# Another order for the steps of the tree block, between the scan and the layers

## The chip, the cores and the metric

The kernel runs on one core of a Trainium2 chip. The metric is the device time of one execution in microseconds, the median of three runs. The core has five engines with a queue of instructions each: TensorE (PE, matrix products), VectorE (DVE), ScalarE (ACT), GpSimd (POOL), and SyncE (SP), which here only starts transfers. An engine takes its instructions strictly in the order in which the program wrote them; between engines only semaphores hold. So an instruction whose input is late holds up everything written behind it on the same engine, ready or not. That is what this case is about.

## The reference, cut to what matters

Four blocks, each `x = x + layernorm(block(layernorm(x)))`, on 2048 tokens (8 sequences of 256) of width 128:

```python
x = x + _layernorm(_L0_attn_ref(_layernorm(x), ...))   # selective scan ("Mamba"), then a norm with gain and bias
x = x + _layernorm(_L0_ffn_ref(_layernorm(x), ...))    # the tree block
x = x + _layernorm(_L1_attn_ref(_layernorm(x), ...))   # four retention layers
x = x + _layernorm(_L1_ffn_ref(_layernorm(x), ...))    # eight experts, one chosen per token
```

The tree block, which the change reorders:

```python
gate = sigmoid(q_flat @ routers.T)                     # 255 gates per token
for level in range(8):                                 # 256 leaf probabilities, products along the paths
    g = gate[:, n - 1:2 * n - 1]
    lp = lp * stack([1 - g, g])
ret = leaf_prob @ leaf_values
out = ret @ Wout_w.T + Wout_b
```

## The kernel before, in words

The 2048 tokens are worked on in four groups of 512 (g = 0 to 3). The scan runs from about 100 us to 280 us of the span. Then comes the list `OPENING`: all steps of the tree block for the four groups, and behind them, interlaced, the first steps of the first retention layer. Each entry is (step, part, group). Every engine walks through the same list and issues its own part of a step, if it has one. So the list alone sets each engine's order: the four engines' programs differ from it only by leaving steps out.

The list is the sorted list of the times `g + t`, where `t` comes from a table: `TREE_SCHEDULE` (L193) for the tree steps, `SCHEDULE` (L173), shifted by 13.25, for the layer's. The numbers have no meaning to the chip. They are only sorted.

The steps of one group, in the order in which each needs the one before it. In brackets the engines and the lines:

- `y_proj` (PE L1230), `t1` (DVE adds, and takes means and variances, L894 to L898; POOL makes reciprocal roots, L519, L521): the end of the scan block.
- `g_norm` (DVE L1017, L1021), `g_stats` (DVE statistics, POOL L528 to L533), `o_norm` (ACT normalises, L757; POOL adds to X, L607).
- `b_stats` (DVE, POOL L528 to L533), `b_norm` (ACT L757), `b_turn` (PE transposes, L1223; ACT copies out, L771).
- `logits` (PE L1372, eight passes; ACT sigmoid, L775), `low_levels` (POOL, levels 0 to 4 of the tree, L592 to L446; in group 0 a memset follows, L600), `levels` (DVE, levels 5 to 7, L444 and L446).
- `lp` (PE transposes the leaves, L1384; ACT copies out, L779), `b_proj` (PE L1230; DVE adds the bias, L1041).
- `t2_stats` (DVE, POOL), `t2_norm` (ACT L757; POOL adds to X, L610), `rx_stats` (DVE, POOL), `rx_norm` (ACT L757).
- Then the first layer: `stats1` and `norm1` (DVE L909, POOL L519, L521), `turn1` (PE L1223, ACT L792), `rotate` (PE L1416, DVE L1076), `spread` (POOL L624, ACT L814), `gate`, `keys`, `scores` (PE L1445, DVE L1091), `values`, `states`, `mix` (PE L1472 ends it), `gather` (ACT L826), `heads` (PE L1480, DVE L1107 to L1111), `var` (DVE L1115, L1117; POOL L629), `unit` (DVE L1122), and so on.

Two waits matter beside those of data. PE's first `rotate` waits until DVE has added the bias of all four groups (`pe.wait_ge(t2_ready, G)`), because it writes to the same PSUM banks. And PE's `b_turn` and `logits` wait for ACT to have emptied their banks, two groups back. After `OPENING` the layers go on in the order `LAYER`, which the change doesn't touch.

Of the kernel before, what the change touches and what calls it, by code (L numbers as in the profile page):

```python
# [180 lines left out]
def layer_order():  # L181
# [9 lines left out]


TREE_SCHEDULE = (  # L193
    (-0.363, "y_proj"), (1.902, "t1"), (4.537, "g_norm"), (4.577, "g_stats"), (5.451, "o_norm"), (6.325, "b_stats"),
    (6.568, "b_norm"), (7.126, "b_turn"), (7.946, "logits"), (7.780, "low_levels"), (8.920, "levels"), (9.756, "lp"),
    (10.296, "b_proj"), (11.612, "t2_stats"), (11.986, "t2_norm"), (12.840, "rx_stats"), (12.992, "rx_norm"),)
FIRST_STEPS_AT, FIRST_STEPS_SCALE = 13.25, 1.00
TREE_STEPS = {what for _, what in TREE_SCHEDULE}
OPENING = [(what, k, g, 0) for _, what, k, g in sorted(
# [1426 lines left out]
```

## Time and profile before

| what | value |
|---|---|
| median of 3 runs | 772.23 us (769.97 to 772.78) |
| the profiled execution's own time | 776.75 us |
| its span | 774.7 us |
| PE busy | 657.1 us, 85% |
| DVE busy | 621.8 us, 80% |
| POOL busy | 428.7 us, 55% |
| ACT busy | 415.2 us, 54% |

The share of busy time is an average over stages with different limits. The page's chain of waits is no help here: it follows the last instruction back and its shares round to 0% on every engine. The timelines of the single engines are what can be read. A row of a timeline gives the start and the length of a group of instructions, and in square brackets how long the engine idled before it and who ended that.

### The profile page before, as it was taken

The numbers are of one execution on the slowest core, as the hardware profiler recorded it, in microseconds if no ns is written. First come the engines' busy times: TensorE is split into PE (matmuls) and PEld (weight loads), VectorE is DVE, ScalarE is ACT, GpSimd is POOL, SyncE is SP. The second block draws the span as 40 slices with busy tenths as digits, with TensorE's granted clock in tenths as the row PEclk, the third lists the DMA queues.
The fourth block names the chain that finished last, engine by engine and source line by source line (L and its number), as shares of the span: only waits on it lengthen the run. The fifth ranks groups of instructions, "written<-read, shape, count | busy, mean of one in ns | idle before, by whom it ended". The sixth has DMA issues, their size and how long they took to land. (4 is left out here: it accounts for less than half of the span.)

```text
span 774.7 us, 13076 instructions
## 1 busy us (share of the span) xinstructions
PE 657.1 (85%) x4791; PEld 438.3 (57%) x4800; DVE 621.8 (80%) x1519; ACT 415.2 (54%) x729; POOL 428.7 (55%) x380
## 2 busy tenths in 40 slices
PE   3997798898988863657889999999999999788894
PEld 1435444444444442554667777777777777566673
DVE  6479898998989857376778888888888888768686
ACT  1996776785767506445545444444444444444451
POOL 6113587795877747655565555555555556443112
PEclk9997799999999995697999999999999999999997
DMA  9003133333333300000000000000000000000001
GB/s 323 10 5 54 34 100 87 89 99 82 76 89 81 81 2 0 0 1 0 2 1 22 2 5 15 22 2 4 15 22 1 6 16 2 1 1 0 1 27 30
DMA packets 17296, 27.34 MB, mean 35 GB/s; under 512 B 2320, under 2 KB 7056, under 8 KB 16976
## 3 DMA queue, kind: packets, MB, share of 16 engines
q1 hardware_dynamic: 17232, 26.51, 12.5%
q8 instruction: 38, 0.62, 0.3%
q14 instruction: 26, 0.21, 0.1%
HBM read 25.32 MB, written 1.18 MB: 34 GB/s over the span
## 5 line engine op out<-in xcount | busy, mean ns | idle before, releaser
L582 POOL TENSOR_TENSOR arena<-arena 128x1024 f32<-128x1024 f32 x64 | 149.9, 2360 | 56.7 <-PE psum L1331 39.4
L1000 DVE TENSOR_TENSOR_SCAN arena<-arena,psum 128x1024 f32<-128x1024 f32 x64 | 142.1, 2269 | 4.2 <-PE psum L1314 2.3
L1331 PE MATMUL psum<-arena,Cs 128*128 128x512 f32 x256 | 125.3, 613 | 1.2 <-POOL arena L582 1.2
L519 POOL TENSOR_TENSOR ve<-mv,eps 128x4 f32<-128x4 f32 x52 | 15.9, 305 | 181.7 <-DVE mv L898 181.7
L714 ACT ACTIVATE arena<-arena 128x510 f32<-128x510 f32 x128 | 84.8, 710 | 54.2 <-DVE arena L1000 52.3
L629 POOL TENSOR_TENSOR arena<-arena,mhalf 128x32 f32<-128x32 f32 x16 | 86.8, 5426 | 2.4 <-DVE arena L1117 2.4
L1331 PEld LDWEIGHTS psum<-arena,Cs 128*128 128x128 f32 x256 | 46.3, 196 | 47.5 <-issue 36.0
L1223 PE MATMUL psum<-Cs,arena 128*128 128x128 f32 x240 | 40.4, 294 | 37.4 <-ACT arena L757 23.2
L1223 PEld LDWEIGHTS psum<-Cs,arena 128*128 128x128 f32 x240 | 29.3, 149 | 56.9 <-ACT arena L757 24.6
L1416 PE MATMUL psum<-arena,Wl 128*128 128x512 f32 x128 | 60.2, 614 | 1.6 <-issue 1.6
L1230 PEld LDWEIGHTS psum<-Wl,arena 128*128 128x128 f32 x384 | 46.6, 191 | 20.9 <-DVE arena L1126 13.3
L1230 PE MATMUL psum<-Wl,arena 128*128 128x128 f32 x384 | 49.7, 279 | 10.0 <-DVE arena L1126 10.0
L1314 PE MATMUL psum<-Cs,arena 128*128 128x128 f32 x256 | 37.0, 293 | 23.5 <-ACT arena L736 20.6
L1314 PEld LDWEIGHTS psum<-Cs,arena 128*128 128x128 f32 x256 | 31.9, 151 | 42.4 <-issue 37.4
L521 POOL TENSOR_TENSOR rs<-ve,mhalf 128x4 f32<-128x4 f32 x52 | 52.6, 1012 | 4.1
L736 ACT ACTIVATE arena<-arena 128x256 f32<-128x256 f32 x128 | 54.1, 493 | 0.0
L894 DVE BATCH_NORM_STATS2 st<-arena 128x6 f32<-128x128 f32 x208 | 45.2, 280 | 3.6 <-ACT arena L757 2.3
L1230 PEld LDWEIGHTS psum<-Wd,arena 128*128 128x128 f32 (+1 forms) x320 | 40.4, 195 | 12.1 <-issue 7.9
L624 POOL TENSOR_TENSOR arena<-arena 128x512 f32<-128x512 f32 x32 | 45.8, 1450 | 2.6 <-DVE arena L1076 2.6
L838 ACT ACTIVATE arena<-psum,Lnc 128x512 f32<-128x512 f32 x16 | 12.4, 778 | 64.4 <-PE psum L1223 64.4
L1206 DVE SCALAR_TENSOR_TENSOR arena<-psum,arena 128x128 f32<-128x128 f32 x128 | 35.9, 344 | 13.0 <-PE psum L1230 11.5
L909 DVE TENSOR_SCALAR arena<-arena,mv,rs 128x128 f32<-128x128 f32 x160 | 44.6, 342 | 1.7 <-POOL rs L521 1.7
(172 smaller groups left out, 1395.5 us busy)
## 6 DMA issues: line engine op xcount, KB each, us to landing
arena<-c_rows_by_state SPq DMA_DIRECT2D x32, 512.0 KB, 4.8
Wl<-wl SPq DMA_DIRECT2D x4, 384.0 KB, 3.1
Wd<-wd SPq DMA_DIRECT2D x1, 1100.0 KB, 10.8
X<-x SPq DMA_DIRECT2D x4, 256.0 KB, 6.7
Sel<-sel SPq DMA_DIRECT2D x1, 1024.0 KB, 8.7
Wl<-wl SPq DMA_DIRECT2D x4, 256.0 KB, 2.8
out<-X SPq DMA_DIRECT2D x4, 256.0 KB, 2.3
Cs<-const SPq DMA_DIRECT2D x1, 614.0 KB, 9.4
```

What stands on the lines that cost most here:

```text
L521: pool.tensor_tensor(rs[:, g * GT:(g + 1) * GT], ve[:, g * GT:(g + 1) * GT], mhalf[:, 0:GT], ALU.pow).then_inc(rstd_ready, 1)
L582: pool.tensor_tensor(Hc[:, h], Hs[:, r, h], Crows[:, r], ALU.mult).then_inc(hc_ready, 1)
L624: pool.tensor_tensor(dst[:, half], halves[:, 0, half], halves[:, 1, half], ALU.add).then_inc(summed.sem, 1)
L629: pool.tensor_tensor(gst[:, cols], gst[:, cols], mhalf[:], ALU.pow).then_inc(rstd_ready, 1)
L714: ins = act.activation(Da[:, h, group(e)].rearrange(seq, s=S)[:, :, 1:], Dt[:, h, group(g)].rearrange(seq, s=S)[:, :, 1:], ACT.Exp, scale= ...
L736: ins = act.activation(Wslot[n % 2][:, part, k, :], Flip[g % 2][:, k * 256:(k + 1) * 256], ACT.Identity, scale=Bt_rows[:, column:column + 1])
L1000: dve.tensor_tensor_scan(Hs[:, turn % 2, h], Da[:, h], rows_of(turn, h), 0.0, ALU.mult, ALU.add).then_inc(scanned, 1)
L1223: ins = pe.transpose(dst[:, tile(k)], src3[:, g * GT + k, :], ident)
L1230: ins = pe.matmul(dst[:, k * width:(k + 1) * width], r[:, tile(k)], w, start=i == 0, stop=i == len(rows) - 1)
L1314: ins = pe.transpose(rows[:, tile(e * GT + k)], Wslot[slot % 2][:, e, k, tile(h)], ident)
L1331: ins = pe.matmul(bank[h], ident, Hc[:, h, group(e)], start=False, stop=False, skip_group_check=True)
L1416: pe.matmul(claim(what, k, layer, g), Wl[:, WL["qk"]][:, tile(k)], Ht[:, group(g)], start=True, stop=True).then_inc(proj.sem, 1)
```

## The change

`TREE_SCHEDULE` has other numbers. Nothing else is changed: the instructions are the same, with the same tiles, and only the order within each engine's queue differs. The new table has one line more, so every line number below it is one higher in the changed kernel. The table begins so, before and after:

```diff
 TREE_SCHEDULE = (
-    (-0.363, "y_proj"), (1.902, "t1"), (4.537, "g_norm"), (4.577, "g_stats"), (5.451, "o_norm"), (6.325, "b_stats"),
+    (0.519, "y_proj"), (1.829, "t1"), (4.728, "g_norm"), (4.819, "g_stats"), (5.661, "o_norm"), (6.453, "b_stats"),
```

ACT, at the tree's start, before. L757 from `X` is `b_norm`, L757 from `arena` is `o_norm`, L771 the copy of `b_turn`, L775 the sigmoid of `logits`, L779 the copies of `lp`. The twelve rows run from the copy of `b_turn` 0 to the copies of `lp` 0.

```order
L771 COPY arena<-psum 128x512
L757 ACTIVATE arena<-arena,shift,rs 128x128 x4
L757 ACTIVATE arena<-X,shift,rs 128x128 x4
L775 ACT_TABLE_LOAD
L775 ACTIVATE arena<-psum 128x512 x2
L771 COPY arena<-psum 128x512
L757 ACTIVATE arena<-arena,shift,rs 128x128 x4
L757 ACTIVATE arena<-X,shift,rs 128x128 x4
L775 ACTIVATE arena<-psum 128x512 x2
L771 COPY arena<-psum 128x512
L757 ACTIVATE arena<-X,shift,rs 128x128 x4
L779 COPY arena<-psum 128x512 x2
```

The same place of the changed kernel (L758, L772, L776 and L780 are those lines):

```order
L758 ACTIVATE arena<-arena,shift,rs 128x128 x4
L772 COPY arena<-psum 128x512
L776 ACT_TABLE_LOAD
L776 ACTIVATE arena<-psum 128x512 x2
L758 ACTIVATE arena<-X,shift,rs 128x128 x4
L758 ACTIVATE arena<-arena,shift,rs 128x128 x4
L772 COPY arena<-psum 128x512
L776 ACTIVATE arena<-psum 128x512 x2
L758 ACTIVATE arena<-X,shift,rs 128x128 x4
L780 COPY arena<-psum 128x512 x2
L772 COPY arena<-psum 128x512
L776 ACTIVATE arena<-psum 128x512 x2
```

The sigmoid of a group now stands ahead of the next group's `b_norm`, where it stood behind it. `o_norm` of group 2 stands ahead of the first `b_turn` copy, `b_norm` of group 1 and `o_norm` of group 3 stand behind the first sigmoid. On PE `lp` of group 0 goes ahead of `b_turn` 2, and `b_proj` 0 and `lp` 1 ahead of `b_turn` 3. POOL's order is the same all through the tree block.

DVE, where the tree's last bias sum meets the layer's first norm, before. L1041 is the bias sum of `b_proj` 3, L894 from `X` is `rx_stats` 1, from `arena` are `stats1` 0 and `t2_stats` 2, L909 is `norm1` 0, L1076 `rotate` 0:

```order
L1041 TENSOR_TENSOR arena<-psum,Wb 128x512
L894 BN_STATS st<-arena 128x6 x4
L896 MEMSET scratch 128x1
L898 BN_AGGR mv<-st 128x2 x4
L894 BN_STATS st<-arena 128x6 x4
L896 MEMSET scratch 128x1
L898 BN_AGGR mv<-st 128x2 x4
L909 TENSOR_SCALAR arena<-arena,mv,rs 128x128 x4
L894 BN_STATS st<-X 128x6 x4
L896 MEMSET scratch 128x1
L898 BN_AGGR mv<-st 128x2 x4
L1076 TENSOR_TENSOR arena<-psum,Cs 128x512 x4
```

And after, from `t2_stats` 2 on:

```order
L895 BN_STATS st<-arena 128x6 x4
L897 MEMSET scratch 128x1
L899 BN_AGGR mv<-st 128x2 x4
L910 TENSOR_SCALAR arena<-arena,mv,rs 128x128 x4
L895 BN_STATS st<-X 128x6 x4
L897 MEMSET scratch 128x1
L899 BN_AGGR mv<-st 128x2 x4
L1042 TENSOR_TENSOR arena<-psum,Wb 128x512
L1077 TENSOR_TENSOR arena<-psum,Cs 128x512 x4
```

The last bias sum (L1041, now L1042) stood ahead of all this and now stands right ahead of `rotate` 0, behind `norm1` 0 and `rx_stats` 1. That of group 2 has moved in the same way, from ahead of `t2_stats` 1 to behind `rx_stats` 0.

POOL, where the first layer's `var` 0 (L629) meets `rx_stats` 3 (L528 to L533) and `spread` (L624), before:

```order
L629 TENSOR_TENSOR arena<-arena,mhalf 128x32
L528 TENSOR_TENSOR ve<-mv,eps 128x4
L529 TENSOR_TENSOR shift<-zeros,mv 128x4
L531 TENSOR_TENSOR rs<-ve,mhalf 128x4
L533 TENSOR_TENSOR shift<-shift,rs 128x4
L624 TENSOR_TENSOR arena<-arena 128x512 x2
```

And after, L529 to L534 being `rx_stats` 3:

```order
L529 TENSOR_TENSOR ve<-mv,eps 128x4
L530 TENSOR_TENSOR shift<-zeros,mv 128x4
L532 TENSOR_TENSOR rs<-ve,mhalf 128x4
L534 TENSOR_TENSOR shift<-shift,rs 128x4
L630 TENSOR_TENSOR arena<-arena,mhalf 128x32
L625 TENSOR_TENSOR arena<-arena 128x512 x2
```

The four small operations of `rx_stats` 3 stand ahead of the root of `var` 0 instead of behind it. DVE's part has moved in the same way. `rx_stats` 2 has moved ahead of the second `scores` of group 0 on DVE.

## Rows read from the trace of the kernel before

**Rows 1.** Stretch, length, PE, PEld, DVE, ACT, POOL busy (count), PEclk, DMA share, GB/s.
```profile
290.00:352.57 62.57, 30.77 (x149) 25.39 (x149) 39.43 (x182) 30.58 (x67) 42.27 (x100) 0.69 0.00 1
...
400.00:660.00 260.00, 251.90 (x2784) 192.78 (x2784) 224.09 (x613) 125.40 (x211) 146.92 (x95) 1.00 0.04 10
```

**Rows 2.** Timeline of ACT, 302 to 339 us: start, length, what, idle before.
```profile
302.81 1.65 ACT L757 ACTIVATE arena<-arena,shift,rs 128x128 f32<-128x128 f32 x4
...
306.27 1.28 ACT L775 ACT_TABLE_LOAD   x1
...
315.93 1.65 ACT L757 ACTIVATE arena<-X,shift,rs 128x128 f32<-128x128 f32 x4 [5.28 <-POOL shift L533]
317.49 1.05 ACT L775 ACTIVATE arena<-psum 128x512 f32<-128x512 f32 x2
...
323.99 1.65 ACT L757 ACTIVATE arena<-X,shift,rs 128x128 f32<-128x128 f32 x4 [4.62 <-POOL shift L533]
...
326.49 1.08 ACT L775 ACTIVATE arena<-psum 128x512 f32<-128x512 f32 x2
...
332.68 0.60 ACT L775 ACTIVATE arena<-psum 128x512 f32<-128x512 f32 x1 [0.26 <-PE psum L1372]
...
338.35 1.65 ACT L757 ACTIVATE arena<-arena,shift,rs 128x128 f32<-128x128 f32 x4 [2.38 <-POOL shift L533]
```

**Rows 3.** Timeline of PE, 301 to 353 us.
```profile
301.18 1.12 PE L1223 MATMUL psum<-Cs,arena 128*128 128x128 f32 x4 [16.01 <-ACT arena L757]
302.97 3.78 PE L1372 MATMUL psum<-Wrq,arena 128*128 128x256 f32 x8 [0.68 <-ACT arena L771]
...
318.54 1.92 PE L1384 MATMUL psum<-Cs,arena 128*128 128x128 f32 x8
...
325.69 0.79 PE L1223 MATMUL psum<-Cs,arena 128*128 128x128 f32 x4 [2.35 <-ACT arena L757]
326.64 3.40 PE L1230 MATMUL psum<-Wlv,arena 128*128 128x128 f32 x16 [0.16 <-ACT arena L779]
...
330.75 1.89 PE L1372 MATMUL psum<-Wrq,arena 128*128 128x256 f32 x8
332.48 1.95 PE L1230 MATMUL psum<-Wlv,arena 128*128 128x128 f32 x16
...
352.57 2.04 PE L1416 MATMUL psum<-arena,Wl 128*128 128x512 f32 x2 [0.92 <-issue]
```

**Rows 4.** Timelines of POOL and DVE, 308 to 315 us.
```profile
308.73 0.20 POOL L592 TENSOR_TENSOR arena<-ones,arena 128x4 f32<-128x4 f32 x1 [1.25 <-ACT arena L775]
...
311.74 0.29 DVE L444 TENSOR_TENSOR arena<-arena 128x128 f32<-128x128 f32 x1 [4.61 <-POOL arena L446]
...
314.04 0.72 DVE L446 TENSOR_TENSOR arena<-arena 128x512 f32<-128x512 f32 x1
```

**Rows 5.** Two stretches with another granted clock; columns as in rows 1.
```profile
322.40:325.80 3.40, 1.05 (x5) 0.62 (x4) 2.12 (x4) 1.81 (x5) 1.48 (x2) 0.96 0.00 0
325.80:329.20 3.40, 3.24 (x16) 2.87 (x17) 0.00 (x0) 2.24 (x5) 1.20 (x6) 0.54 0.00 0
```

**Rows 6.** Timeline of DVE, 343 to 351 us.
```profile
343.55 0.69 DVE L1041 TENSOR_TENSOR arena<-psum,Wb 128x512 f32<-128x512 f32 x1 [0.88 <-PE psum L1230]
...
350.34 0.86 DVE L894 BATCH_NORM_STATS2 st<-X 128x6 f32<-128x128 f32 x4
```

**Rows 7.** Timelines of POOL, ACT, PE and DVE, 383 to 394 us.
```profile
383.09 5.43 POOL L629 TENSOR_TENSOR arena<-arena,mhalf 128x32 f32<-128x32 f32 x1 [2.35 <-DVE arena L1117]
388.48 0.20 POOL L528 TENSOR_TENSOR ve<-mv,eps 128x4 f32<-128x4 f32 x1
...
390.67 2.48 POOL L624 TENSOR_TENSOR arena<-arena 128x512 f32<-128x512 f32 x2
...
390.75 1.65 ACT L757 ACTIVATE arena<-X,shift,rs 128x128 f32<-128x128 f32 x4 [6.96 <-POOL shift L533]
...
392.92 0.66 PE L1480 MATMUL psum<-Cs,arena 128*128 128x128 f32 x4 [2.24 <-ACT arena L826]
...
393.61 0.69 DVE L1107 TENSOR_REDUCE arena<-psum 128x32 f32<-128x512 f32 x1 [4.32 <-PE psum L1480]
```

More of the change, by code:

```diff
@@ L193 @@
 TREE_SCHEDULE = (
-    (-0.363, "y_proj"), (1.902, "t1"), (4.537, "g_norm"), (4.577, "g_stats"), (5.451, "o_norm"), (6.325, "b_stats"),
-    (6.568, "b_norm"), (7.126, "b_turn"), (7.946, "logits"), (7.780, "low_levels"), (8.920, "levels"), (9.756, "lp"),
-    (10.296, "b_proj"), (11.612, "t2_stats"), (11.986, "t2_norm"), (12.840, "rx_stats"), (12.992, "rx_norm"),)
+    (0.519, "y_proj"), (1.829, "t1"), (4.728, "g_norm"), (4.819, "g_stats"), (5.661, "o_norm"), (6.453, "b_stats"),
+    (7.238, "b_norm"), (7.973, "b_turn"), (8.202, "logits"), (8.299, "low_levels"), (9.328, "levels"),
+    (9.813, "lp"), (10.784, "b_proj"), (11.604, "t2_stats"), (11.914, "t2_norm"), (12.693, "rx_stats"),
+    (13.007, "rx_norm"),)
 FIRST_STEPS_AT, FIRST_STEPS_SCALE = 13.25, 1.00
```

## The prediction

> **What bounds the kernel now.** I read the busy times by stretch first, then the timeline of each engine over the tree block, then the granted clock there, last the timelines around 390 us. From 290 to 352.57 us, the stretch that is reordered up to the first `rotate`, no engine is the bound: POOL, the busiest, works 42.3 of 62.6 us and PE 30.8. From 400 to 660 us PE works 251.9 of 260 us [rows 1]. So the tree block is a chain of waits between four engines, and what it gives up or takes moves the PE-bound layers behind it by the same amount: their order and their work stay as they are.
>
> In the tree block the reader is to see where ACT stands still with work ready behind it. At 315.93 ACT has waited 5.28 us for POOL's shift, to do `b_norm` 2. Behind it stands the sigmoid of group 1, which starts only at 317.49. At 323.99 it is the same: 4.62 us of wait for the shift of `b_norm` 3, with the copies of `lp` 0 and the sigmoid of group 2 (326.49) behind it [rows 2]. This late sigmoid makes POOL's `low_levels` 2 late, but what counts most is the last one. Sigmoid 3 ends at 332.68 + 0.60 = 333.28. POOL then has the low levels of group 3, and only behind them, in its fixed order, `t2_stats` 0, for whose shift ACT waits until 338.35 [rows 2]. From there one chain of group 0 runs through `t2_norm`, `rx_stats`, `rx_norm`, `stats1`, `norm1` and `turn1` to `rotate` at 352.57 [rows 3]. POOL's order is not changed, so the end of sigmoid 3 is the point by which the tree block is to be judged.
>
> **The change, part by part.** All times are on the clock of the profiled execution of before.
>
> First group. ACT now does `o_norm` 2 (1.65 us) ahead of the copy of `b_turn` 0. It started at 302.81 behind that copy and could have started little before, since POOL's shift had just come; I take 302.6. It ends at 304.3, and the copy (about 0.6, a sigmoid's length) at 304.9, where it was done by 302.97, when PE began: 1.9 later [rows 2, 3]. The logits take 3.78 at the low clock [rows 3] and end at 308.7. The table load (1.28 us [rows 2]) waits for nothing and lies beside them. The second sigmoid ends at 309.3. Before, POOL started on it at 308.73 [rows 4]. So group 0 is 0.6 late: low levels 309.3 to 312.3 (3.0, from 308.73 to 311.74), `levels` 312.3 to 315.3 (3.0, from 311.74 to 314.76) [rows 4].
>
> Second group. `b_norm` 1 now follows the sigmoid: 309.3 to 311.0, 4.7 later than before. Transposes 1.12 [rows 3], to 312.1. Meanwhile ACT does `o_norm` 3, to 312.6, then the copy, to 313.2. Logits 3.78, to 317.0. The sigmoid isn't queued behind a wait any more and ends at 317.6. Before, it ended at 317.49 + 1.05 = 318.54 [rows 2]. The group has lost 4.7 us and still comes out 0.9 earlier, since the head start was spent waiting.
>
> Third group. Shift 2 comes 0.6 late, as the low levels before it, at 316.5, ahead of need. `b_norm` 2 runs 317.6 to 319.2. PE turns the leaves of group 0 meanwhile, 317.0 to 318.9 at the low clock (1.92 [rows 3]). `b_turn` 2 and its copy: 320.7 at the high clock (0.79), 321.0 at the low (1.12) [rows 3]. Logits 1.89 or 3.78 [rows 3]: 322.6 or 324.8. Sigmoid 2 ends at 323.2 or 325.4, before at 327.57 [rows 2].
>
> Fourth group. Shift 3 is due on POOL behind the low levels of group 1, which start at 317.75 instead of 318.6, so at 323.1 instead of 323.96 [rows 2]. `b_norm` 3 comes behind sigmoid 2 and ends at 324.9 or 327.1. PE fills the time with `b_proj` 0 (1.95 at the high clock [rows 3]) and `lp` 1 (about 1.0, half of 1.92), from 322.6 to 325.5 or from 324.8 to 327.7. Then `b_turn` 3 (0.79), copy (0.6), logits (1.89), sigmoid (0.6): 325.5 + 3.9 = 329.4, or 327.7 + 3.9 = 331.6. Before: 333.28 [rows 2]. So the tree term is **-3.9 us** if logits 2 run at 2.4 GHz and **-1.7 us** if they run at 1.2 GHz. I take -3.0, nearer the first: in the new order PE is busy from 313.2 to 318.9 almost without a break just before.
>
> From there to `rotate` 0 the same steps lie in the same order, but for the bias sums. The sum of group 3 (0.69) was done at 343.55 in idle time. Now it stands behind `rx_stats` 1, which starts at 350.34 and takes 1.2 [rows 6]. So it would run from 351.55 to 352.25, and PE's `rotate`, which waits for it, started at 352.57 [rows 3]. It fits with 0.3 us to spare: cost 0, the cover being `turn1` on PE and ACT. If `rx_stats` 1 slips by more than 0.3, every further 0.1 counts. From above, the whole sum and its statistics would cost 0.69 + 1.2 = 1.9; from below nothing can be gained. The sum of group 2 moves behind `rx_stats` 0, where DVE waits for ACT's `rx_norm` anyway: 0.
>
> `rx_stats` 2 ahead of the second `scores`: DVE does the same two pieces in the other order ahead of the same third one, and `mix`, the next to need the mask, comes later. 0.
>
> `rx_stats` 3. Before, its POOL part stood behind the root of `var` 0 (5.43 us from 383.09), its shift came at 390.7, and ACT did `rx_norm` 3 from 390.75 to 392.3, with `gather` 1 behind it. PE had finished `mix` 1 at 392.92 - 2.24 = 390.68 and stood 2.24 us; DVE stood 4.32 [rows 7]. Now the shift comes 2.2 us (388.48 to 390.67) after DVE's 383.3, ACT does `rx_norm` 3 in its idle 6.96 us, `gather` runs from 390.7 to 391.3 and `heads` 1 start at 391.35: 1.57 earlier. The price is the root, which moves behind the four small operations: 385.4 to 390.9, and `spread` (390.67) starts at 390.9, 0.2 later [rows 7]. ACT's copies for `scores` hang on that, so not all of the 1.57 comes through. Alone `gather` would let them follow directly. Bounds 0 and -1.6, I take **-1.1**.
>
> **Sum.** -3.0 - 1.1 = -4.1 us. The profiled execution's own time is 776.75, so 772.65. That execution is 4.5 above the median of the runs shown, and the change is the same in both: 772.23 - 4.1 = **768.1 us**.
>
> **The clock.** What decides inside the tree term is PE's clock. Between 322.4 and 325.8 the granted clock was 0.96, nearly all of it at 2.4 GHz, while PE worked 1.05 us of 3.4. Then it was 0.54, nearly all at 1.2 GHz, though PE was busy for 3.24 of the next 3.4 us [rows 5]. The same `b_proj` took 3.40 in it and 1.95 later [rows 3]. The break before the fall that the row shows was 2.35 us [rows 3]. In the new order the breaks after 313.2 are a few tenths to 1.2 us, and no such break is left until the last leaves.
> The Trainium skill speaks against a change that spreads PE's work out at the start (TensorE: Matmul & The Clock Gate, section Why this matters for your kernels): breaks between bursts of matmuls take the clock down, and it advises to keep them short. The trace agrees, with 3.40 against 1.95 for the same products.
> By that rule the new breaks at 302 to 313 (2.6, 2.4 and 1.1 us by the times above) keep the clock low longer; by the trace it was low there before as well. What it would do later is the first rival.
>
> **Rivals.**
> 1. The clock stays low through logits 2 and `b_proj` 0. Tree term: -1.7 + (3.40 - 1.95) = -0.3; with -1.1 that is 770.8. For it: the first logits come in two separate bursts. Against: PE is busier from 317 on than before. Chance 0.17.
> 2. The gain at 390 us doesn't come, since the root of `var` 0 and `spread` are what `scores` 2 wait for: only -3.0, 769.2. Chance 0.1.
> 3. Slower. The low clock holds from the first logits to the last: logits 2 to 324.8, `b_proj` 0 to 328.2, `lp` 1 to 330.1, `b_turn` 3 to 331.2, copy 331.8, logits 3 to 335.6, sigmoid 336.2. That is 2.9 later than 333.28; with -1.1 it is +1.8, and with `rx_stats` 1 slipping as well up to +1.9 more: 774.0, at most 776. It decides as soon as sigmoid 3 ends 1.1 later than before. For it: `b_turn` 1 is 4.7 late. Against: busy times like those here brought the clock up before. Chance 0.07.
> 4. Nothing comes through, because another step of the chain to `rotate` 0 is bound by something that hasn't moved: 772.2. In the trace each step there waits for the one before. Chance 0.08.
>
> **How the numbers follow.** The forecast has 0.58, with 766.5 to 770.1 as its own range: the two ends of the tree term with the -1.1, -5.0 and -2.8, and 0.7 of scatter in a median of three, a quarter of the 2.8 between the runs shown. A difference of under 0.5%, 3.9 us here, can't be told from none. Of the forecast two thirds lie below 768.4, which is 0.38, and a third of rival 2, 0.03, and 0.02 for a gain that I don't see: faster 0.43. Slower by over 0.5% needs the far end of rival 3: 0.05. The rest, 0.52, is the same. The range runs from 766.0 to 772.3, with rivals 1, 2 and 4 in it and rival 3 outside.
>
> **What would show it.** Right: sigmoid 1 ends at about 317.6 with no ACT wait for a shift ahead of it; logits 2 take 1.9; sigmoid 3 ends at 329.4 to 331.6; `rotate` 0 starts near 349.6 right behind `turn1`; DVE's last bias sum ends before it; ahead of `heads` 1 PE stands under 1 us. Wrong: a logits row of 3.8 us after 320; a wait of PE for DVE's L1042 ahead of `rotate` 0; ACT waiting for a shift with a sigmoid behind it; a break of over 1.5 us between the two kernels' starts of the layers that isn't there at 353.

## The result, and the profile after

The changed kernel takes 768.59 us (median of 18 runs, 765.06 to 770.12), the kernel before 771.54 (18 runs beside them). The ratio is 0.9953, with a 95% interval of 0.9935 to 0.9971: 3.6 us less by the ratio, 2.95 by the two medians. The interval lies below 1, so the change does save time; the gain is just under the half percent up to which the prediction speaks of the same. A gain of 4.1 us was forecast. The same kernel in a second set (12 runs, experiment e7 below) came out at 0.9972 (0.9957 to 0.9987), 2.2 us less by the ratio.

| | before | after |
|---|---|---|
| median | 771.54 | 768.59 |
| profiled execution, own time | 776.75 | 769.43 |
| its span | 774.7 | 767.6 |
| PE, DVE, POOL, ACT busy | 657.1, 621.8, 428.7, 415.2 | 651.6, 622.2, 429.2, 415.3 |

The two traces differ by 7.1 us of span, twice what the times say. So distances, and not absolute times, have to be compared. The first transposes of the tree block (`b_turn` 0) start at 301.18 before and at 299.42 after. These 1.76 us lie in the scan, whose code and order are the same in both, so they are no gain of the change: in the thirteen traces used here `b_turn` 0 starts anywhere from 294.9 to 301.2. Another 1.7 us of the 7.1 lie behind `heads` 14, again in the same code and order; that stretch takes 122.5 to 127.0 us over the thirteen traces. I count from `b_turn` 0. Busy time by stretch, as in [rows 1]:

```profile
290.00:352.57 62.57, 34.54 (x154) 26.09 (x155) 39.06 (x173) 33.06 (x73) 42.99 (x100) 0.69 0.00 1
...
400.00:660.00 260.00, 249.67 (x2785) 191.97 (x2787) 222.22 (x610) 124.25 (x209) 149.03 (x94) 0.99 0.04 10
```

The first window is that of before, and the layer begins 5 us earlier here. In the stretch that matches it, 288.24 to 347.56, PE works 29.5 of 59.3 us and POOL 42.0. So in the tree block no engine is the bound, as before, and in the layers PE is. Timeline of ACT, answering to [rows 2]:

```profile
300.85 1.65 ACT L758 ACTIVATE arena<-arena,shift,rs 128x128 f32<-128x128 f32 x4 [1.49 <-POOL shift L534]
302.40 0.56 ACT L772 COPY arena<-psum 128x512 f32<-128x512 f32 x1
...
306.83 0.60 ACT L776 ACTIVATE arena<-psum 128x512 f32<-128x512 f32 x1 [1.11 <-PE psum L1373]
...
314.84 0.60 ACT L776 ACTIVATE arena<-psum 128x512 f32<-128x512 f32 x1 [1.11 <-PE psum L1373]
315.33 1.64 ACT L758 ACTIVATE arena<-X,shift,rs 128x128 f32<-128x128 f32 x4
...
321.65 0.60 ACT L776 ACTIVATE arena<-psum 128x512 f32<-128x512 f32 x1 [1.11 <-PE psum L1373]
322.14 1.63 ACT L758 ACTIVATE arena<-X,shift,rs 128x128 f32<-128x128 f32 x4
...
328.03 0.60 ACT L776 ACTIVATE arena<-psum 128x512 f32<-128x512 f32 x1 [0.26 <-PE psum L1373]
...
333.51 1.65 ACT L758 ACTIVATE arena<-arena,shift,rs 128x128 f32<-128x128 f32 x4 [2.19 <-POOL shift L534]
```

The waits of 5.28 and 4.62 us for POOL's shift are gone: `b_norm` 2 and 3 (315.33 and 322.14) follow their sigmoids without a wait. What ACT waits for now, between the sigmoids, is PE. One wait for a shift is left at the start, 1.49 us ahead of `o_norm` 2, with the copy of `b_turn` 0 behind it. Timeline of PE, answering to [rows 3]:

```profile
299.42 1.11 PE L1224 MATMUL psum<-Cs,arena 128*128 128x128 f32 x4 [16.01 <-ACT arena L758]
303.01 3.78 PE L1373 MATMUL psum<-Wrq,arena 128*128 128x256 f32 x8 [2.49 <-ACT arena L772]
...
318.45 3.16 PE L1373 MATMUL psum<-Wrq,arena 128*128 128x256 f32 x8 [0.78 <-ACT arena L772]
321.41 2.50 PE L1231 MATMUL psum<-Wlv,arena 128*128 128x128 f32 x16
...
326.00 1.99 PE L1373 MATMUL psum<-Wrq,arena 128*128 128x256 f32 x8 [0.78 <-ACT arena L772]
...
347.56 6.50 PE L1417 MATMUL psum<-arena,Wl 128*128 128x512 f32 x8 [0.91 <-DVE arena L1042]
```

Logits 2 ran partly at the low clock in this execution: 3.16 us, between 1.9 and 3.8, with a granted clock of 0.61 from 318.45 to 321.60. DVE's moved bias sums:

```profile
337.75 0.66 DVE L1042 TENSOR_TENSOR arena<-psum,Wb 128x512 f32<-128x512 f32 x1
...
345.33 0.86 DVE L895 BATCH_NORM_STATS2 st<-X 128x6 f32<-128x128 f32 x4
...
346.53 0.66 DVE L1042 TENSOR_TENSOR arena<-psum,Wb 128x512 f32<-128x512 f32 x1
```

And the timelines of POOL, ACT, PE and DVE around `heads` 1, answering to [rows 7]:

```profile
380.86 5.43 POOL L630 TENSOR_TENSOR arena<-arena,mhalf 128x32 f32<-128x32 f32 x1
386.25 2.94 POOL L625 TENSOR_TENSOR arena<-arena 128x512 f32<-128x512 f32 x2
...
380.94 1.65 ACT L758 ACTIVATE arena<-X,shift,rs 128x128 f32<-128x128 f32 x4 [1.43 <-POOL shift L534]
...
387.10 0.66 PE L1481 MATMUL psum<-Cs,arena 128*128 128x128 f32 x4 [0.70 <-ACT arena L827]
...
390.10 0.63 PE L1224 MATMUL psum<-Cs,arena 128*128 128x128 f32 x4 [1.48 <-DVE arena L1112]
...
386.32 1.74 DVE L1123 TENSOR_TENSOR arena<-arena 128x512 f32<-128x512 f32 x1 [1.91 <-POOL arena L630]
387.98 0.68 DVE L1108 TENSOR_REDUCE arena<-psum 128x32 f32<-128x512 f32 x1
```

PE stands 0.70 instead of 2.24 us ahead of `heads` 1 (L1481). In its place one wait is new and one is longer: DVE's `unit` 0 waits 1.91 us for the later root, and then takes 1.74 us beside POOL's `spread`; PE waits 1.48 us for DVE's L1112, where it was 0.96 before.

The points of the chain, each as its distance from `b_turn` 0 in the trace, before and after, in us. `heads` are DVE's (L1107), the end of rotate 0 is that of DVE's fourth product:

| point | before | after | difference | second trace after (e7) |
|---|---|---|---|---|
| sigmoid 0 ends | 7.48 | 8.01 | +0.53 | +0.53 |
| sigmoid 1 ends | 17.36 | 16.02 | -1.34 | -1.34 |
| sigmoid 2 ends | 26.39 | 22.83 | -3.56 | -4.73 |
| sigmoid 3 ends | 32.10 | 29.21 | -2.89 | -4.54 |
| rotate 0 starts | 51.39 | 48.14 | -3.25 | -4.46 |
| rotate 0 ends | 57.89 | 55.37 | -2.52 | -4.09 |
| heads 1 | 92.43 | 88.56 | -3.87 | -5.44 |
| heads 2 | 110.96 | 107.43 | -3.53 | -5.10 |

From there to `heads` 14 the difference stays within 0.1 us in the first trace and in e7's. In others it changes by up to 0.6 us (e5's, from -3.60 to -3.04).

### The profile page after: what moved, and what is told of

Same layout as the page of the kernel before. It is cut to its first block and busy times, and to the rows that moved or that the text cites. A ratio compares the mean times of both kernels' runs of the same rounds, so it can differ in the third digit from the quotient of the medians.

```text
span 767.6 us, 13076 instructions
## 1 busy us (share of the span) xinstructions
PE 651.6 (85%) x4791; PEld 434.7 (57%) x4800; DVE 622.2 (81%) x1519; ACT 415.3 (54%) x729; POOL 429.2 (56%) x380
## 5 line engine op out<-in xcount | busy, mean ns | idle before, releaser
L1077 DVE TENSOR_TENSOR arena<-psum,Cs 128x512 f32<-128x512 f32 x64 | 40.3, 688 | 5.2 <-PE psum L1417 5.2
```

## The experiments

All ratios are against the kernel before, run on the same chip. They were run in three sets of four.

**e1: the tree block's moves alone.**

```diff
+put_ahead(('rx_stats', 0, 2, 0), ('states', 0, 0, 0))
+put_ahead(('rx_stats', 0, 3, 0), ('states', 0, 1, 0))
```

(in the changed kernel, behind the list `OPENING`; `put_ahead` takes an entry out and puts it ahead of another)

> The changed kernel with rx_stats 2 and 3 put back where they stood (behind the second scores of their layer group and behind var 0). My theory: two separate gains, some 2.5 us in the tree block and some 1 us ahead of heads 1. So here the tree gain alone: 2.5 us below the kernel before (ratio 0.9968), rotate 0 early as in the changed kernel, but ACT's rx_norm 3 again ahead of gather 1 and PE idle 2.2 us ahead of heads 1. Rival (the whole gain is the tree's, the move of rx_stats is neutral): 3.6 us below before.

Measured: 767.25 us, ratio 0.995 (0.9932 to 0.9968), 3.9 us less and as good as with the moves of `rx_stats`. In the trace sigmoid 3 ends 4.66 us earlier than before, counted from `b_turn` 0, the rotate ends 4.46 earlier, and from `heads` 0 to `heads` 2 it takes 36.2 us as before (35.2 in the changed kernel). So the tree moves carry all of the gain that the times show.

**e2 and e8: `rx_stats` 3 alone.**

```diff
+put_ahead(('rx_stats', 0, 3, 0), ('var', 0, 0, 0))
```

(in the kernel before; the same kernel twice)

> The kernel before with one move alone: rx_stats 3 ahead of var 0 (on DVE and POOL). My theory: 1.0 us below before; PE idle ahead of heads 1 down from 2.24 to 0.7, heads 1 on PE 1.5 earlier, of which about 0.5 is given back because unit 0 and so out_turn 0 wait for the root of var 0. Rival: 0, because the root that now comes 2 us later decides instead.

> The kernel before with rx_stats 3 alone ahead of var 0, once more. Its first trace shows 35.2 us from heads 0 to heads 2 where before shows 36.2, but its times came out 0.1% above before, in two clusters, 768 to 770 and 772 to 775. Theory: the 1.0 us is real and the upper cluster is a fall of the clock somewhere, which the move doesn't cause: ratio 0.9985 or within 0.2% of it, and the same 35.2 us. Rival: the later root brings a break of PE in which the clock falls more often, which costs what the move gains: ratio again 1.000 or above, and if the trace is of the upper cluster, a low clock near heads 1.

Measured: e2 772.21 us, ratio 1.001 (0.9989 to 1.003); e8 771.36 us, ratio 0.9996 (0.9972 to 1.002). One execution of e8, the profiled one, took 3655 us. The cause isn't known, and its trace is not used. In e2's trace `heads` 0 to 2 take 35.2 us, 1.0 less than before. That distance is 36.2 in the traces of before, e1 and e9, without the move, and 35.2 in the nine with it (e3, also without it, had 38.6 with the fall of the clock shown below). So the 1.0 us is in every trace, and the times don't show it: e8's interval includes 0.9987, e2's just does not.

The granted clock of the single executions, averaged over their span, shows more. Divided at 0.952, the executions of e2 and e8 without the one of 3655 us, and the 75 of the kernel before in the three sets, fall so:

| | at 0.952 or less | median of these | above 0.952 | median of these |
|---|---|---|---|---|
| before | 17 of 75 | 774.0 us | 58 | 770.7 us |
| e2 and e8 | 15 of 23 | 772.3 us | 8 | 768.4 us |

At a like clock the kernel with the move is about 2 us faster, but most of its executions run at the lower clock, and that can eat the gain. It speaks for e8's rival. With the tree moves it points the same way: e1's five executions, without the move, have 0.954 to 0.955, and the 37 of the changed kernel, e7 and e10, with it, have 0.943 to 0.952. Where in the span the clock is lost, and whether the later root does it, is not shown: e2's trace is one of the high clock (0.957).

**e3: only the two sigmoids ahead of the waits.**

```diff
+put_ahead(('logits', 0, 1, 0), ('b_norm', 0, 2, 0))
+put_ahead(('b_turn', 0, 2, 0), ('b_norm', 0, 3, 0))
+put_ahead(('logits', 0, 2, 0), ('b_norm', 0, 3, 0))
```

(in the kernel before)

> The kernel before with two moves alone: the sigmoid of group 1 ahead of b_norm 2, and logits 2 with its sigmoid ahead of lp 0 and b_norm 3. Nothing of groups 0 and 1 is delayed as in the changed kernel. If the two sigmoids queued behind a wait for a shift are the whole tree gain: sigmoid 3 ends 2.9 us earlier against the first transposes than before, time 2.5 us below before. My theory gives a little less, 1.5 us, since b_proj 0 and lp 1 still stand behind b_turn 3 on PE and lp 0's copies behind b_norm 3 on ACT.

Measured: 770.87 us, ratio 0.9997 (0.9977 to 1.0016). In the trace sigmoid 3 is 1.61 us earlier than in the trace of before, but only 0.26 earlier than in e2's, whose tree block has the old order. The two are not alike in the clock, though. Logits 2 took 2.23 us in e2's trace, and here the full 3.78, behind a break of 5.68 us:

```profile
314.15 1.11 PE L1233 MATMUL psum<-Cs,arena 128*128 128x128 f32 x4 [5.68 <-ACT arena L767]
315.94 3.78 PE L1382 MATMUL psum<-Wrq,arena 128*128 128x256 f32 x8 [0.68 <-ACT arena L781]
```

So up to 1.5 us of what the sigmoids gave may have gone to the clock in this execution. Windows of e3 around `heads` 1, columns as in [rows 1]:

```profile
382.70:389.50 6.80, 4.33 (x81) 2.88 (x79) 2.41 (x6) 3.55 (x8) 4.90 (x7) 0.94 0.01 2
389.50:396.30 6.80, 6.30 (x45) 5.66 (x47) 4.80 (x17) 3.67 (x7) 1.54 (x2) 0.56 0.00 0
```

The clock fell to the lower level at 389.5, behind the break of 2.24 us ahead of `heads` 1, and `heads` 1 to 2 took 20.96 us instead of 18.53. The same break, as long, is in the trace of before, and there it stayed high:

```profile
388.10:394.90 6.80, 4.10 (x81) 2.88 (x79) 2.42 (x6) 3.78 (x8) 4.89 (x7) 1.00 0.01 2
```

So by time the sigmoids alone bring nothing. Whether that is because they gain little, or because this order loses to the clock what it gains, one trace can't tell.

**e9: the sigmoids, and `lp` and `b_proj` ahead of the next `b_turn`.**

```diff
+put_ahead(('logits', 0, 1, 0), ('b_norm', 0, 2, 0))
+put_ahead(('lp', 0, 0, 0), ('b_turn', 0, 2, 0))
+put_ahead(('b_turn', 0, 2, 0), ('b_norm', 0, 3, 0))
+put_ahead(('lp', 0, 0, 0), ('b_turn', 0, 2, 0))
+put_ahead(('logits', 0, 2, 0), ('b_norm', 0, 3, 0))
+put_ahead(('b_proj', 0, 0, 0), ('b_turn', 0, 3, 0))
+put_ahead(('lp', 0, 1, 0), ('b_turn', 0, 3, 0))
```

(in the kernel before)

> The kernel before with PE's and ACT's new order from logits 1 on (sigmoid 1 ahead of b_norm 2, lp 0 ahead of b_turn 2, b_proj 0 and lp 1 ahead of b_turn 3, sigmoid 2 ahead of b_norm 3), but the old one ahead of it, so groups 0 and 1 are not delayed, and DVE and POOL as before. Theory: the tree gain of the changed kernel comes from these moves and not from the early ones, which only cost 0.5 us at sigmoid 0; sigmoid 3 is 3 to 4.5 us earlier against the first transposes than before, 2.5 to 3 us in time, ratio 0.9965. Rival: the sigmoids moved alone brought nothing in time (ratio 0.9997), and so won't these: above 0.9985.

Measured: 767.61 us, ratio 0.995 (0.9928 to 0.9973). Its interval doesn't meet e3's. So these moves, from logits 1 on, are the change's gain; `o_norm` 2 ahead of the first copy and DVE's moves add nothing that shows. Its trace is one with a low clock for logits 2, 3.78 us, as in e3's. Between these two, alike in that, sigmoid 3 is 0.97 us earlier here; the ratios are 3.6 us apart, and the rest is in neither trace. Sigmoid 3 is 2.57 us earlier than before:

```profile
302.91 1.99 PE L1386 MATMUL psum<-Wrq,arena 128*128 128x256 f32 x8 [1.58 <-ACT arena L785]
308.54 1.91 PE L1398 MATMUL psum<-Cs,arena 128*128 128x128 f32 x8 [3.63 <-DVE arena L460]
311.36 1.11 PE L1237 MATMUL psum<-Cs,arena 128*128 128x128 f32 x4 [0.92 <-ACT arena L771]
313.15 3.78 PE L1386 MATMUL psum<-Wrq,arena 128*128 128x256 f32 x8 [0.68 <-ACT arena L785]
316.73 2.99 PE L1244 MATMUL psum<-Wlv,arena 128*128 128x128 f32 x16
```

**e10: DVE's bias sums back.**

```diff
+put_ahead(('b_proj', 0, 1, 0), ('t2_stats', 0, 0, 0))
+put_ahead(('b_proj', 0, 2, 0), ('t2_stats', 0, 1, 0))
+put_ahead(('b_proj', 0, 3, 0), ('stats1', 0, 0, 0))
```

(in the changed kernel)

> The changed kernel with DVE's three moved bias sums (b_proj 1, 2, 3) back where they stood; PE, ACT and POOL as changed. Theory: they cost and bring nothing, PE starts rotate 0 at the same distance behind turn1 0 (2.0 us): ratio as the changed kernel, 0.995 to 0.997. Rival: the last sum right ahead of the rotate holds it by some tenths of a microsecond: then rotate 0 starts up to 0.3 us earlier here.

Measured: 767.35 us, ratio 0.9932 (0.9905 to 0.996), not to be told from the changed kernel's. The start of the rotate is 2.00 us behind `turn1` 0 in both (343.55 to 345.55 here, 345.56 to 347.56 there). The row of PE names DVE's sum as what ended its wait in the changed kernel (0.91), and here nothing (0.92, "issue"), at the same distance: a name alone doesn't make a wait.

**e4: PE kept busy ahead of the first layer.**

```diff
+                if (step[0], step[2]) == ("turn1", 0):
+                    pe.wait_ge(gated, 2 * G)
+                    keep_busy(bank[2], 12)
```

(in the changed kernel, in PE's loop over its steps; the definition of `keep_busy` is cut. It issues so many products of 128x256 whose result is read by nobody. The rows show each as two passes: x24 is 12 products.)

> The changed kernel with 12 more products of 128x256 on PE (their result is read by nobody) ahead of turn1 0, in the 6.9 us in which PE idles there. Theory: PE's granted clock fell in that idle time, so the first rotate ran at 1.2 GHz (6.5 us for 8 passes against 3.6 later). With PE busy there the clock stays at 2.4 GHz, the rotate takes about 3.7 and the layers start 2.5 us earlier: 2.5 us below the changed kernel, ratio to before about 0.992. Rival: DVE's four sums and the bias sum bind the rotate, not the clock: under 0.7 us.

Measured: 767.95 us, ratio 0.9936 (0.9912 to 0.996). In its trace:

```profile
334.87 5.34 PE L1508 MATMUL psum<-Wrq 128*128 128x256 f32 x24
341.93 0.63 PE L1224 MATMUL psum<-Cs,arena 128*128 128x128 f32 x4 [1.72 <-DVE arena L910]
343.61 3.70 PE L1417 MATMUL psum<-arena,Wl 128*128 128x512 f32 x8 [1.05 <-DVE arena L1042]
```

The first rotate takes 3.70 instead of 6.50 us, and from its start to DVE's fourth product it takes 4.43 instead of 7.23: 2.8 us in these two traces, as the theory has it, and the rival falls there. By time it was less: 4.9 us below before, where the changed kernel had 3.6, with intervals that overlap. The trace is that of the fastest execution. The three fastest, 761.2 to 763.9 us, had a granted clock of 0.959 to 0.965 over their span; the other eight, 765.3 to 769.4, had 0.952 to 0.956, near the changed kernel's 0.948 to 0.952. So in most executions the products seem to have held the clock up only a little.

**e5: PE kept busy at the start of the tree block.** 28 such products ahead of `b_turn` 0, 4 ahead of logits 0 and 3 ahead of `b_turn` 1, in bank 7.

```diff
+            busy = {('b_turn', 0): 28, ('logits', 0): 4, ('b_turn', 1): 3}
+                if (step[0], step[2]) in busy:
+                    keep_busy(bank[7], busy[step[0], step[2]])
```

(in the changed kernel, in PE's loop over its steps, like e4's; lines between these are cut)

> The changed kernel with 35 more products of 128x256 on PE (read by nobody) where it idles at the start of the tree block: 28 ahead of the first transposes, 4 ahead of logits 0, 3 ahead of b_turn 1. Theory: the clock then stays at 2.4 GHz from the end of the scan, logits 0 and 1 take 1.9 us each instead of 3.8, sigmoid 3 ends 2.8 us earlier against the first transposes than in the changed kernel, and the time falls by 2.5 us (ratio to before about 0.992). Rival: POOL's low levels, its memset and its statistics bind from sigmoid 0 on, and at most the 1.9 us of logits 0 come through; or the tree block doesn't care and it is 0.

Measured: 768.63 us, ratio 0.9966 (0.9942 to 0.999): nothing gained on the changed kernel. The trace says why:

```profile
308.80 2.00 PE L1373 MATMUL psum<-Wrq,arena 128*128 128x256 f32 x8 [1.35 <-ACT arena L772]
311.38 1.09 PE L1385 MATMUL psum<-Cs,arena 128*128 128x128 f32 x8 [0.58 <-DVE arena L447]
314.20 1.11 PE L1224 MATMUL psum<-Cs,arena 128*128 128x128 f32 x4 [1.73 <-ACT arena L758]
315.99 3.78 PE L1373 MATMUL psum<-Wrq,arena 128*128 128x256 f32 x8 [0.68 <-ACT arena L772]
```

Logits 1 went fast (2.00) and sigmoid 1 ended 3.47 us earlier than before. Then PE had to wait for `levels` and for `b_norm` 2, the clock fell (0.93 from 311.0 to 314.2, then 0.50 to 320), and logits 2 took 3.78: all of it was given back. Sigmoid 3 is 2.92 us earlier than before, where the changed kernel has 2.89 in its first trace and 4.54 in its second. The products ahead of logits 0 also ran over their break at the low clock (3.62 us together) and held it up.

**e6: both.** The products of e5 and e4, with 14 ahead of `turn1` 0 and one ahead of the first rotate.

```diff
+            busy = {('b_turn', 0): 28, ('logits', 0): 4, ('b_turn', 1): 3}
+                    keep_busy(bank[7], busy[step[0], step[2]])
+                if (step[0], step[2]) == ("turn1", 0):
+                    keep_busy(bank[2], 14)
+                if (step[0], step[2]) == ("rotate", 0):
+                    keep_busy(bank[2], 1)
```

(in the changed kernel; lines between these are cut)

> The additional products of e5 and those of e4 together, with 14 instead of 12 ahead of turn1 0 and one ahead of the first rotate. Theory: both add up, 5 us below the changed kernel, ratio to before 0.989. The runs of e4 lay in two clusters, 761 to 766 and 768 to 769; if that is the clock falling in the gap in some executions, the two more products make the upper cluster smaller. Rival: the gains overlap, no better than the better of the two.

Measured: 762.52 us, ratio 0.9915 (0.9887 to 0.9944). In the trace sigmoid 3 is 6.12 us earlier than before and the rotate's end 8.01. The clusters are 760.8 to 765 (six runs) and 769 (two). By the ratios of the same set it is 4.4 us below the changed kernel (e7). Alone, e4 gave 1.3 us and e5 0.5 by their ratios; e6 also has three more products than the two together, and what share is theirs wasn't tested.

**e11: products in all larger breaks, in the changed order.**

```diff
+            busy = {('b_turn', 0): 35, ('logits', 0): 2, ('b_turn', 1): 4,
+                    ('logits', 1): 1, ('b_turn', 2): 1, ('logits', 2): 1}
```

(the rest as e6)

> The changed kernel with additional products (read by nobody) in all larger breaks of PE: 35 ahead of b_turn 0, 2 ahead of logits 0, 4 ahead of b_turn 1, 1 each ahead of logits 1, b_turn 2, logits 2, 14 ahead of turn1 0, 1 ahead of the first rotate. Theory: the clock stays at 2.4 GHz through the whole tree block, which it didn't in e5 and e6; logits 0 to 3 take 1.9 to 2.0 us each, sigmoid 3 is 2 us earlier than in e6 at best, and the time is 1 us below e6: ratio 0.990. Rival: it falls somewhere all the same, ratio as e6, 0.9915.

Measured: 763.36 us, ratio 0.9881 (0.9847 to 0.9915), 9.2 us below before by the ratio, products and new order together. Of that the new order alone has 2.2 to 5.2 us (0.9972, 0.9953 and 0.9932 in e7, the result and e10). It has the lowest ratio of all versions, but its interval meets e6's. The clock still fell once, in logits 2:

```profile
311.90 3.47 PE L1373 MATMUL psum<-Wrq,arena 128*128 128x256 f32 x8 [0.34 <-ACT arena L772]
...
340.70 3.70 PE L1417 MATMUL psum<-arena,Wl 128*128 128x512 f32 x8 [0.62 <-DVE arena L1042]
```

**e12: the same in e9's order, with `rx_stats` 3 ahead of `var` 0.**

```diff
+            busy = {('b_turn', 0): 35, ('b_turn', 1): 2, ('lp', 0): 6, ('b_turn', 2): 2, ('logits', 2): 1}
```

(the products ahead of the layers as in e6; in the kernel before with e9's and e2's moves)

> The order of e9 with rx_stats 3 ahead of var 0, and additional products in PE's breaks as they lie in that order (35 ahead of b_turn 0, 2 ahead of b_turn 1, 6 ahead of lp 0, 2 ahead of b_turn 2, 1 ahead of logits 2, 14 ahead of turn1 0, 1 ahead of the first rotate). Theory: with the clock up, groups 0 and 1 come 2 to 4 us earlier than in the changed kernel's order, but POOL's low levels, memset and statistics then bind; sigmoid 3 is 0.5 us earlier than in e11: ratio 0.9895. Rival: the earlier groups only wait for POOL, same as e11.

Measured: 765.64 us, ratio 0.9898 (0.9854 to 0.9943). Sigmoid 3 is 5.02 us earlier than before, in e11 5.28. What the theory was about didn't come to pass: groups 0 and 1 were hardly earlier than e11's. Sigmoid 0 ended 7.47 us behind `b_turn` 0 (e11 6.22), sigmoid 1 12.23 (e11 12.44), since logits 1 ran at the low clock behind a break of 2.22 us:

```profile
308.38 3.58 PE L1387 MATMUL psum<-Wrq,arena 128*128 128x256 f32 x8 [2.22 <-ACT arena L786]
```

So whether earlier groups would only wait for POOL stays untested. e11's and e12's intervals overlap, so which is faster stays open.

**e7: the changed kernel once more**, with no edit.

> The changed kernel once more, for a second trace and more times beside e8 on the same chip. Theory: order fixes every distance but those that the clock changes; so from the first transposes to sigmoid 3 the distance differs from the first trace by up to 1.9 us with the place of the low clock (29.2 us there), and from the first heads to the third it is 35.2 us again. Ratio 0.995. Rival: the differences between executions lie elsewhere.

Measured: 767.88 us, ratio 0.9972 (0.9957 to 0.9987). From `b_turn` 0 to the end of sigmoid 3 it takes 27.56 us, where the first trace had 29.21; `heads` 0 to 2 is 35.2 again. Of the 1.65 us, 1.16 are there when sigmoid 2 ends: logits 2 ran at 2.4 GHz here, with a granted clock of 1.00 from 316 to 319:

```profile
316.62 1.99 PE L1373 MATMUL psum<-Wrq,arena 128*128 128x256 f32 x8 [0.71 <-ACT arena L772]
```

## Why the prediction was right, point by point

- **The bound.** Right. The tree block was a chain of waits; what it gave up was still there in the PE-bound layers (-3.5 at `heads` 2, within 0.1 us the same to `heads` 14).
- **First group**, +0.6: +0.53. **Second**, -0.9: -1.34; `b_norm` 1, `o_norm` 3 and the copy follow each other a little closer than I added up. **Third**, -2.2 to -4.4 by the clock: -3.56 with the clock rising in the middle of logits 2, -4.73 with it high.
- **Sigmoid 3**, the tree term, -1.7 to -3.9, -3.0 taken: -2.89. With the clock high it is -4.54 to -4.70 (e7, e10, e1, e4), more than my far end, against the one trace of before. The old order has its own spread: e2's trace, the same tree block, is 1.35 us below the first one at sigmoid 3. Between e2's trace (logits 1 and 2 in 1.99 and 2.23 us) and e7's (3.78 and 1.99) the change is worth 3.2 us.
- **The bias sums**, 0: right (e10). The 0.3 us of room that I worked out was enough.
- **From there to the rotate's end.** This term I left out. The rotate itself, from PE's start to DVE's fourth product, took 6.50 us before and 7.23 after; over all traces without additional products 5.97 to 7.23. It depends on the granted clock there (0.63 from 350.5 to 359.1 before, 0.54 from 345.56 to 354 after), and took 0.7 back in the first trace.
- **`rx_stats` 3**, -1.57 at `heads` 1 and -1.1 net: -1.35 and -1.01 in the trace. The size was right in the trace, the reason for the price wrong: I had `spread` and ACT's copies hold the rest, but `spread` starts 0.14 us earlier behind `heads` 0 than before. It is the root of `var` 0, which DVE's `unit` 0 waits for, ahead of `heads` 1 in its queue: PE's `heads` 1 are 1.54 earlier behind `heads` 0, DVE's part 1.35, and L1110 behind it takes 0.53 instead of 0.18. In the times this term hasn't been seen (e1, e2, e8); the lower clock of most executions with the move is the likely reason.
- **The sum**, -4.1: -3.6 by the first set and -2.2 by the second, -3.5 in the trace. That it came so near is partly luck. By time the tree term alone is worth 3.9 us (e1), more than the 3.0 taken, and the `rx_stats` term, taken at 1.1, doesn't show (e1, e2, e8). Two misses in opposite directions gave a good sum.
- **The rivals.** The low clock through logits 2 (the first) occurs, in e9's and e5's traces, and costs 1.6 to 2 us against e7's at sigmoid 3. The time that this rival gave doesn't come with it: the tree term is still -2.57 and -2.92 there, not -0.3. The second, that the gain at `heads` 1 doesn't come, is refuted by the traces and unrefuted by the times. The slower one didn't occur, and neither did the fourth, that nothing comes through: `rotate` 0 starts 3.25 us earlier.
- **The signs.** Two that the prediction named came out the other way. Logits 2 took 3.16 us in the first trace instead of 1.9. And PE's row names DVE's L1042 ahead of `rotate` 0 (0.91), which was to be a sign of being wrong; e10 shows that it is none.
- What I called the mechanism, a sigmoid queued behind a wait for a shift, isn't shown to be enough. e3 takes just that away and gains nothing in time; e9, with `lp` and `b_proj` pulled ahead as well, gains it all. How much of the difference is PE's work done in the meantime and how much is e3's clock stays open. In my sum this was there as "PE fills the time with `b_proj` 0 and `lp` 1", without a price of its own.

The Trainium skill (TensorE: Matmul & The Clock Gate, section Why this matters for your kernels) advises to keep the breaks between bursts of matmuls short. The runs agree: 12 useless products in a break of 6.88 us made the rotate behind it 2.8 us shorter in the trace, and products in all larger breaks took the ratio to 0.9881, where the new order alone has 0.9932 to 0.9972.

## What to carry to other kernels

In a stage where no engine is the bound, look for the instruction that stands ready in an in-order queue behind a wait for something else, but price also what the other engines can do in that time: here the gain showed only with the two together. Count the clock of TensorE as a term of such a stage, for what is moved and for the stage behind it, and compare traces by distances from a common point, since two executions of one program differ by more than such a change brings. Look at the granted clock of every execution too, not only at that of the profiled one: a gain that each trace shows can be lost in the executions at a lower clock. Where PE idles ahead of work on the critical path, products that nobody reads, in a free PSUM bank, can be worth as much as a better order.

## What the runs showed of the hardware

- The same break of PE (2.24 us ahead of `heads` 1) was followed by a fall of the granted clock to 1.2 GHz in e3's trace and by none in those of before, e1 and e9. In each case the instructions and their distances from `heads` 0 on were the same. The fall cost 2.4 us.
- Ahead of `b_turn` 3, PE broke off for 2.35 us in the trace of before and for 3.22 us in e2's. Behind the shorter break `b_proj` 0 took 3.40 us, behind the longer one 2.05. So the length of the break alone didn't decide.
- Where the clock is low moves one and the same order by up to 1.7 us within the tree block (sigmoid 3 at 29.21 and 27.56 us behind `b_turn` 0), nearly half of the measured change.
- DVE's 128x512 product of `unit` 0 took 1.74 us in the nine traces with `rx_stats` 3 moved, where it ran beside POOL's `spread`, and 0.68 in the four without (before, e1, e3, e9), where POOL had nothing of 512 columns to do.
